# Attention scores of one head as one 32-row product on its own row group of TensorE, with the mask as a key row, in a fused cross-attention and expert kernel

## The reference, cut to what matters

```python
# x (64,128,128), ctx (64,120,128), mask (64,120); 16 heads of 8 dimensions, 8 experts of width 512
n = layernorm(x)
q, k, v = (n @ Wq + bq), (ctx @ Wk + bk), (ctx @ Wv + bv)         # split into 16 heads
score = einsum('bhqd,bhkd->bhqk', q, k) / sqrt(8)
score = where(mask, -1e30, score)
x = x + (softmax(score) @ v) @ Wo + bo
n = layernorm(x)
probs = softmax(n @ Wr.T); the two best of 8 experts, with their shares
x = x + sum over those two of share * (gelu(n @ W1[e] + b1[e]) @ W2[e] + b2[e])
```

## Time and profile before

| | us |
|---|---|
| median of 3 runs | 856.4 |
| lowest and highest run | 851.75, 870.18 |
| the profiled execution, its own time | 863.12 |
| its span, first to last instruction | 861.4 |

### The profile page before, as it was taken

How to read it: one execution, slowest core, us unless ns; L and a number is a source line. 1 busy time by engine, 2 the same in 40 slices (tenths; PEclk the granted TensorE clock), 3 DMA queues, 4 the chain that set the end, 5 groups by cost and what they waited for, 6 DMA issues and landing times.

```text
span 861.4 us, 18252 instructions
## 1 busy us (share of the span) xinstructions
PE 646.0 (75%) x4964; PEld 493.1 (57%) x4964; DVE 554.5 (64%) x1813; ACT 531.5 (62%) x1060; POOL 490.2 (57%) x892
## 2 busy tenths in 40 slices
PE   2677786876877888878978546999898979989400
PEld 1355565665655656655656435887686858767300
DVE  4466677776877778767866543766475656656436
ACT  4367676765866667767767435887576767866300
POOL 8233366655675757656677770675565646566610
PEclk9899999997999999999999758999899999999855
DMA  4666766667567776676665167877575756664068
GB/s 139 182 180 170 212 183 198 180 199 204 166 184 216 203 204 180 196 195 196 169 179 145 52 183 233 268 244 234 177 214 180 225 183 213 202 193 155 4 240 344
DMA packets 118905, 164.24 MB, mean 191 GB/s; under 512 B 22479, under 2 KB 77286, under 8 KB 118823
## 3 DMA queue, kind: packets, MB, share of 16 engines
q1 hardware_dynamic: 107143, 141.87, 56.4%
q0 software_dynamic: 9088, 17.07, 5.8%
q10 hardware_dynamic: 2592, 4.33, 1.3%
HBM read 73.07 MB, written 33.92 MB: 124 GB/s over the span
## 4 chain that ended last, share of the span: by engine, by line
PE 38%; SPq 17%; DMA 16%; issue 13%; POOL 6%; DVE 5%; ACT 2%; another core or an unknown queue 2%; POOLq 0%; DVEq 0%; ACTq 0%
DMA qb<-negm 4%; SPq L330 4%; DMA qb<-dense 4%; PE bank L1260 4%; SPq L312 4%; PE bank L1428 4%; PE bank L1426 3%; PE bank L1427 3%; PE bank L1411 3%; PE bank L1412 3%; PE bank L1414 3%; PE bank L1275 3%; DMA qb<-yd 3%; PE bank L1248 3%; SPq L338 2%
## 5 line engine op out<-in xcount | busy, mean ns | idle before, releaser
L650 POOL DMA_INDIRECT yd<-vs,idt x156 | 159.8, 1025 | 127.9 <-DVE vs L961 81.0
L1009 ACT ACTIVATE pt<-bank,mcol 120x512 f32<-120x512 f32 x256 | 167.9, 687 | 53.4 <-PE bank L1260 43.5
L707 DVE TENSOR_REDUCE mx<-bank 128x4 f32<-128x480 f32 x256 | 159.9, 649 | 46.0 <-PE bank L1248 39.3
L550 POOL DMA_INDIRECT xd<-rows,posi x128 | 128.7, 1005 | 98.2 <-DVE posi L812 68.4
L947 DVE TENSOR_TENSOR qb<-hid,qb 128x512 fp32r<-128x512 f32 x156 | 108.3, 694 | 101.4 <-ACT hid L1142 61.0
L1139 ACT ACTIVATE qb<-bank,btile 128x512 fp32r<-128x512 f32 x156 | 109.2, 700 | 72.4 <-PE bank L1428 42.1
L1260 PE MATMUL bank<-qb,dense 128*120 128x512 f32 x256 | 97.4, 460 | 61.2 <-DMA qb<-negm 50.7
L1248 PE MATMUL bank<-kb,dense 128*128 128x480 f32 x256 | 92.7, 445 | 22.7 <-issue 8.5
L1142 ACT ACTIVATE hid<-bank,btile 128x512 f32<-128x512 f32 x156 | 109.0, 699 | 0.0
L1041 ACT ACTIVATE ots<-bank 128x512 f32<-128x512 f32 x64 | 38.2, 597 | 79.0 <-PE bank L1275 71.0
L1260 PEld LDWEIGHTS bank<-qb,dense 128*120 128x120 f32 x256 | 39.7, 192 | 70.3 <-DMA qb<-negm 56.9
(11 more groups left out here) (169 smaller groups left out, 1559.0 us busy)
## 6 DMA issues: line engine op xcount, KB each, us to landing
kb<-wd SPq DMA_DIRECT2D x40, 512.0 KB
qb<-wd SPq DMA_DIRECT2D x38, 512.0 KB
qb<-dense SPq DMA_DIRECT2D x128, 128.0 KB
dense<-comp SPq DMA_DIRECT2D x64, 248.0 KB
kb<-dense SPq DMA_DIRECT2D x128, 120.0 KB
rows<-xd SPq DMA_DIRECT2D x39, 264.0 KB
wd<-wsp SPq DMA_DIRECT2D x16, 512.0 KB
qb<-yd SPq DMA_DIRECT2D x16, 512.0 KB, 6.2
```

The costliest lines, as they stand in the source:

```text
L550: g.indirect_dma_start(xd, bass.IndirectOffsetOnAxis(ap=posi[r % 4][:, bk:bk + 1], axis=0), rows[r % 4][:, bk // 2, bk % 2, :], None, boun ...
L650: g.indirect_dma_start(yd, bass.IndirectOffsetOnAxis(ap=idt[k][:, j:j + 1], axis=0), yrow[p.parity][:, j, :], None, bounds_check=2 * NTOK ...
L707: v.tensor_reduce(mx[c % 2][:, :, gg, b], wide[m % 2][:, 0:J * KL].rearrange("p (j k) -> p j k", j=J), op=ALU.max, axis=AX.X).then_inc(w_f ...
L1009: a.activation(pt[i % NP][:].rearrange("p j q -> p (j q)"), scores[t % 2][0:KL, :], ACT.Exp, bias=mcol[:, 2 * c + t // G:2 * c + t // G + ...
```

## The change

The block operands `kb` and `qb` are gone, with key_blocks, query_blocks and the zeroing. `dense` is split into `dq` and `dk`, four buffers of each. A head's product now contracts only its own 32 partitions, with `tile_position=(32j, 0)`, so on row group j of the array: 16 matmuls of 120 columns replace 4 by_query matmuls, 16 of 128 columns replace 4 by_key matmuls. A call makes 8 of them, alternating between two row groups, each of which writes its own bank; it waits until both banks have been read. The mask lies in row 11 of `dk` (one DMA, L320 before) and so enters both products, and the exponential has no bias. The maxima go to rows 31 and 15 of `dq`. As `dk` has ones in both rows at all times, row 15 (with 31, 47 and so on) of a reused `dq` is zeroed first by a small DMA (`cleared`). The parts of `comp` are spread by 6 DMAs where 4 did it. The expert stage gets buffers of its own, and its wait for the last by_key is gone. `best` and `exponential` see the same number of elements, with g and j exchanged.

```diff
-    NHI, NLO, MSK = 3, 7, 11
+    MSK, NLO, NHI = 11, 15, 31
-        dense = [sb(f"dense{k}", [P, G, NK], F32R) for k in range(ND)]
-        qb = [sb(f"qb{k}", [P, J, G, N2], F32R) for k in range(2)]
-        kb = [sb(f"kb{k}", [P, J, G, K2], F32R) for k in range(2)]
+        dq = [sb(f"dq{k}", [P, G, N2], F32R) for k in range(ND)]
+        dk = [sb(f"dk{k}", [P, G, K2], F32R) for k in range(ND)]
+        wt = sb("wt", [P, 4, 2, 2, HID], F32R)
+        xThl = sb("xThl", [P, 2, 2, TB], F32R)
+        hhl = sb("hhl", [P, 2, HC, TB], F32R)
...
-            def key_blocks(c):
...
-            def query_blocks(c):
...
+            def prepare(c):
                 if c < ND:
                     sp.wait_ge(dense_set, 2 * (c + 1))
                 else:
                     sp.wait_ge(b_full, 8 * (c - ND + 1))
+                    sp.dma_start(dq[c % ND][NLO::16]..., dq[c % ND][3::16]...).then_inc(cleared[c % ND], 16)
+                sp.dma_start(dk[c % ND][MSK::R]..., maskd...to_broadcast([J, G, K2])).then_inc(mask_row[c % ND], 16)
             def spread_high(c):
                 sp.wait_ge(hi_done, 2 * c + 1)
+                for term in (1, 2):
+                    sp.dma_start(rows_of(dq, c, term), comp[:, QHI]...).then_inc(dn_in[c % 2], 16)
                 sp.wait_ge(hi_done, 2 * c + 2)
+                for term in (0, 2):
+                    sp.dma_start(rows_of(dk, c, term), comp[:, KHI]...).then_inc(dn_in[c % 2], 16)
             def spread_low(c):
                 sp.wait_ge(lo_done, 2 * c + 1)
+                sp.dma_start(rows_of(dq, c, 0), comp[:, QLO]...)
                 sp.wait_ge(lo_done, 2 * c + 2)
+                sp.dma_start(rows_of(dk, c, 1), comp[:, KLO]...)
             def maxima(c):
                 sp.wait_ge(nm_split, 2 * c + 2)
-                sp.wait_ge(qblk[c % 2], 64 * (c // 2 + 1))
...
             def slot(n):                                  # SP
-                if chunk(n + 1):
-                    query_blocks(n + 1)
+                if chunk(n + 3):
+                    prepare(n + 3)
...
-                if chunk(n + 3):
-                    key_blocks(n + 3)
-                    mask_rows(n + 3)
...
-                    sp.wait_ge(b_full, 8 * NCH)           # before the third tile's weights
...
-            v.memset(flat(kb[0], "p j g n").bitcast(F32), 0.0).then_inc(kb_zero, 1)   # and kb[1]
-            clear(qb[0])                                  # ACT, and qb[1]
...
-                a.activation(pt..., scores[t % 2][0:KL, :], ACT.Exp, bias=mcol[:, ...], scale=SCALE)
+                a.activation(pt..., scores[t % 2][0:KL, :], ACT.Exp, scale=SCALE)
...
+            def by_query(c, p):
+                b, half = divmod(p, 2)
+                if p == 0:
+                    pe.wait_ge(dn_in[c % 2], 96 * (c // 2 + 1))
+                    pe.wait_ge(mask_row[c % ND], 16 * (c // ND + 1))
+                    if c >= ND:
+                        pe.wait_ge(cleared[c % ND], 16 * (c // ND))
+                m = 8 * c + 2 * p
+                if m:
+                    pe.wait_ge(w_free, m)
+                for g in range(G):
+                    for k in range(2):
+                        j = 2 * half + k
+                        last = t_.matmul(wide[k][:, g * KL:(g + 1) * KL], dq[c % ND][R * j:R * j + R, g, b * S:(b + 1) * S],
+                                         dk[c % ND][R * j:R * j + R, g, b * KL:(b + 1) * KL], start=True, stop=True, tile_position=(R * j, 0))
+                        if g == G - 1:
+                            last.then_inc(w_full, 1)
+            def by_key(c, p):                             # the same with dk as weights, dq moving,
...                                                       # scores[k], and a wait for exp_done 8c + 2p
             def slot(n):                                  # PE: one call where two matmuls stood
-                by_key(n, 0)
-                by_key(n, 1)
+                by_key(n, 0)
                 if chunk(n - 2):
                     project_out(2 * n - 3)
-                by_query(n + 1, 4)
-                by_query(n + 1, 5)
+                by_query(n + 1, 2)
```

More of the change, by code:

```diff
@@ L44, in turns, with moe_attention @@
         return self.quad * each + (each + more)
-def moe_attention(nc, x, ctx, mask, maskT, Wq, Wk, bqk, Wv, bv, Wo, bo, Wr, W1, b12, W2, out):
+def moe_attention(nc, x, ctx, mask, Wq, Wk, bqk, Wv, bv, Wo, bo, Wr, W1, b12, W2, out):
     S, B, D = x.shape
@@ L104, in moe_attention @@
         bias_qk = sb("bias_qk", [P, 2])
-        ones_k = sb("ones_k", [P, 1])
+        pad_q = sb("pad_q", [P, 1])
+        pad_k = [sb(f"pad_k{i}", [P, 1]) for i in range(3)]
         masku = sb("masku", [B, KL], mask.dtype)
@@ L176, in moe_attention @@
         flat = lambda t, spec: t[:].rearrange(f"{spec} -> p ({spec[2:]})")
[L177 to L182, removed]
+        wtile = [wt[:, k] for k in range(4)]
+        xTh, xTl = ([xThl[:, k, i, :] for k in range(2)] for i in range(2))
         xrow = [rows[k][:].rearrange("p a b w -> p (a b) w") for k in range(4)]
@@ L211, in moe_attention @@
         w_full, w_free = sem("w_full"), sem("w_free")
-        dn_in, qblk, kblk, kfirst, mrow = two("dn_in"), two("qblk"), two("kblk"), two("kfirst"), two("mrow")
+        dn_in, cleared, mrow = two("dn_in"), four("cleared"), two("mrow")
         v_full, v_taken = sem("v_full"), sem("v_taken")
@@ L290, in spread_high @@
                     sp.wait_ge(b_full, 8 * (c - ND + 1))
[L291 to L302, removed]
@@ L304, in key_blocks @@
-            def key_blocks(c):
[L306 to L315, removed]
+                    sp.dma_start(dq[c % ND][NLO::16].rearrange("x g n -> x (g n)").bitcast(F32),
+                                 dq[c % ND][3::16].rearrange("x g n -> x (g n)").bitcast(F32)).then_inc(cleared[c % ND], 16)
@@ L1252, in by_key @@
+            def by_key(c, p):
                 if not chunk(c):
                     return
-                b, g = divmod(t, G)
-                i = 8 * c + t
-                if t == 0:
+                b, half = divmod(p, 2)
+                if p == 0:
                     pe.wait_ge(mrow[c % 2], 32 * (c // 2 + 1))
-                if i >= 2:
-                    pe.wait_ge(exp_done, i - 1)
-                t_.matmul(scores[t % 2][0:KL, :].rearrange("p (j q) -> p j q", j=J), dense[c % ND][:, g, N2 + b * KL:N2 + (b + 1) * KL],
-                          qb[c % 2][:, :, g, b * S:(b + 1) * S], start=True, stop=True).then_inc(b_full, 1)
+                i = 8 * c + 2 * p
+                if i:
+                    pe.wait_ge(exp_done, i)
+                for g in range(G):
+                    for k in range(2):
+                        j = 2 * half + k
+                        last = t_.matmul(scores[k][0:KL, g * S:(g + 1) * S], dk[c % ND][R * j:R * j + R, g, b * KL:(b + 1) * KL],
+                                         dq[c % ND][R * j:R * j + R, g, b * S:(b + 1) * S], start=True, stop=True, tile_position=(R * j, 0))
+                        if g == G - 1:
+                            last.then_inc(b_full, 1)
@@ L1341, in slot @@
                     earlier(n - 4)
-                by_key(n, 2)
-                by_key(n, 3)
-                by_query(n + 1, 6)
-                by_query(n + 1, 7)
+                by_key(n, 1)
+                by_query(n + 1, 3)
                 if chunk(n - 1):
@@ L1352, in slot @@
                     turn_heads(2 * n - 1)
-                by_key(n, 4)
-                by_key(n, 5)
+                by_key(n, 2)
                 if chunk(n + 1):
@@ L1358, in slot @@
                 by_query(n + 2, 0)
-                by_query(n + 2, 1)
                 if chunk(n):
@@ L1365, in slot @@
                     values(n + 1)
-                by_key(n, 6)
-                by_key(n, 7)
-                by_query(n + 2, 2)
-                by_query(n + 2, 3)
+                by_key(n, 3)
+                by_query(n + 2, 1)
                 if chunk(n - 1):
```

102 lines of the change are left out of this document (42 added, 60 removed).

## The result

| | before, us | after, us |
|---|---|---|
| median of 5 runs each, same chip | 857.45 | 943.57 |
| lowest and highest | 851.75, 870.18 | 934.02, 969.00 |
| the profiled execution | 863.12 | 969.00 |

The ratio is 1.095 (95% interval 1.084 to 1.106): the change makes the kernel slower.

What follows compares the result with a forecast made beforehand. SP's queue was taken as the bound, with PE behind it. 32 slots x (13.7 - 12.7) = 32 us and 6 for filling gave -38: 825 us profiled, 818 for the median; range 795 to 880.

Steps and rivals of the forecast that it cites:

- The clock falls: Rival: tiled calls get half clock for a third of each slot, PE needs +3.5 us, about 930 us; chance 0.04.
- the forecast's 12.7: Attention slot length in us: the dense slot's 11.4 plus 1.3 for PE, against a mean of 13.7 before.
- SP, 12.5 to 7.3 us: SP's queue per slot: 5 fewer issues (3.2 us) and 2 us less waiting, so SP stops being the bound.
- Maxima a wait of 0.2 us, put at nothing: Before by_key: maxima land 5.3 us after q high, PE needs them after 5.1; the wait counted as nothing.
- "5.1": Time in us from `high` writing q to the next by_key: 4.45 plus what PE gains in calls.
- Row groups load side by side, 0.45 us a call: PE: weight loads of two row groups overlap, so a call's 8 products take 4 x 0.112 = 0.45 us.
- PE +1.3 us a slot: PE's by_key and by_query calls, with drains and bare loads at mode switches, cost 1.3 us more a slot.
- Filling -6 us: Before the first by_key: by_query starts about 3.7 us sooner and maxima are issued sooner, 6 us gained in all.
- Waits in SP's place: Rival: waits for both banks or late maxima cost 1.0 us a slot, only filling is gained, 850 us; chance 0.17.
- PE busy without a gap in slots above 14: One of the trace signs named in advance as showing the forecast wrong, in the attention slots.
- loads going one by one: Rival: the two row groups' weight loads don't overlap, +3.6 us, slots of 16.3 us, 933 us; chance 0.10.

Runs made afterwards that it cites:

- g5: The changed kernel (after), unedited, run again on the second chip as a control: 862.2 us, ratio 1.047 to before.
- E2: After with each call making two all-row products in place of eight row-group products, scores not the reference's: 760.1 us, ratio 0.930 to before.
- e1: Separate kernel, PE alone running patterns of row-group and all-row products: two groups with 128 columns took 64.8 us at clock 0.53.
- g6: After with each row-group product streaming 240 or 256 columns in place of 120 or 128, half the scores wrong: 811.6 us, ratio 0.987 to before.
- h9: e4 with the keys' spreads issued after the maxima and `earlier` moved behind the second call, third chip: 866.6 us.
- h11: g6 with the same two order edits as h9, third chip: 870.2 us, ratio 1.016 to before.
- h10: e4 unedited, run again on the third chip as a control: 889.4 us, ratio 1.043 to before.
- e4: After with each by_key call and the by_query call behind it merged into 16 products over four row groups, first chip: 780.9 us, ratio 0.954 to before.
- e3: After with one useless all-row product added to each of its 8 calls a slot: 952.8 us, ratio 1.163 to before.
- g7: After with by_query in two all-row products a call and by_key left on row groups: 779.5 us, ratio 0.951 to before.

## Why the prediction was wrong, point by point

The step that failed is the rival "The clock falls", to which I gave 0.04. Its price came out near, by luck: half clock for a third of each slot, +3.5 us, about 930 us. Measured: half clock for 64% of the stage, slots of 16.9 against the forecast's 12.7, so +4.2 us, and 943.6 us. In the prediction's own sum 3.5 us of work take 7.0 of 16.2 us, so half clock would have been 43% of the time. Two errors met: there was more half clock, and less beside it, for with the clock at 1.00 a slot of 16.9 us would come to 16.9 x (1 - 0.64 / 2) = 11.5 us, not 12.7 (an estimate, as if PE bounded all of it). Its chance was wrong, and so were "nothing but the risk" for it, where two of the three stretches of the earlier trace rows already stand at 0.93 and 0.90, and the one piece of evidence against it, "in the dense slot with its tiled `weigh` the clock stays at 1.00". `Weigh` feeds 120 rows into four column groups. It was no neighbour of products that use 32 rows of each of two groups. The rows before held no such product, so what the clock would do was an unknown cost like the others and should have been bounded from both sides. The earlier trace rows had the dear end, a `weigh` of 1.94 us against 1.08; with PE as the bound behind SP, it applies to all of a slot, and such slots took 20.16 us.

The other steps, against the rows of after and g5:

- **SP, 12.5 to 7.3 us: right.** The slot's issues in after, timeline of SP's queue:

```profile
269.38 1.22 SPq L302 DMA_DIRECT2D dq<-comp  x2
270.64 1.50 SPq L305 DMA_DIRECT2D dk<-comp  x2
272.20 1.19 SPq L318 DMA_DIRECT2D dq<-negm  x2
...
276.02 0.83 SPq L292 DMA_DIRECT2D dk<-maskd  x1
```

  From 269.38 to 276.85 are 7.5 us; then SP waits.
- **Maxima a wait of 0.2 us, put at nothing: small, as forecast.** Counted as in the earlier trace rows, they are waited for 7.3 us in all of after and 14.1 in g5, where 14.1 / 32 = 0.4 a slot. The 0.2 itself holds a slip: between 414.04 and 418.49 PE's calls get longer by 0.10 + 0.28, not by the 0.65 behind "5.1", so the sum should have given 4.8 and a wait of 0.5.
- **Row groups load side by side, 0.45 us a call: right** (0.47 for by_key, 0.53 for by_query).
- **PE +1.3 us a slot: too much, if anything.** In g5's slot of 13.05 us the clock of 0.87 means 3.4 us at half, which at full clock would be 1.7: PE is busy 12.69 - 1.7 = 11.0 us, against 10.58 in before's slot at 1.00. That is +0.4 of busy time; drains between matmuls that overlap a modelled end aren't in it. The 13.05 us are near the forecast's 12.7 even with that half clock in them. If all slots were like this one, 31 x 0.8 = 25 us would be gained on the 13.8 of before.
- **Filling -6 us: -2.8.** By_query starts at 20.49 us, 3.4 sooner than in the earlier trace rows, but each call now waits for two reductions, and the maxima are ready only 0.4 us sooner:

```profile
20.49 1.11 PE L1219 MATMUL bank<-dk,dq 32*128 32x120 f32 x8 [1.08 <-DMA dk<-comp]
23.43 1.11 PE L1219 MATMUL bank<-dk,dq 32*128 32x120 f32 x8 [1.83 <-DVE mx L682]
```

- **Waits in SP's place: small.** For exponentials PE waits 1.5 us in all of after and 5.8 in g5, for reductions 4.9 in either. The waits for `taken` are 21.3 us, but they aren't new: in before they are 17.3. E2 has the same waits for two banks and slots of 11.8 us.
- **"PE busy without a gap in slots above 14"** was named as the sign of a wrong forecast, and it is what the trace shows. I had tied it to loads going one by one; the half clock gives the same picture, and only the clock column and the durations of untouched matmuls tell the two apart.

**Shown:** the two-group, 128-column pattern alone takes the clock to half with PE never idle (e1); in the kernel longer streams of the same products bring it from 0.75 to 0.95 and gain 51 us net (g6), without a stall in either run; all-row products, which can't keep the heads apart, keep it at 0.99, and the time is then 7% under before (e2). **Argued only:** what the chip measures when it lowers the clock. **Open:** what stalls the engines in after and in h9 to h11; how much of after's loss (1.095 against g5's 1.047) and of h10's lower clock (0.77 against e4's 0.89) comes from those stalls and how much from the chip otherwise; and why e3's filler brought the clock back so little where g6's columns did.

## What to carry to other kernels

Before splitting an all-row matmul into products on row groups, ask what the new pattern does to the granted clock, and measure the pattern by itself between stretches of all-row work: a busy PE isn't a PE at 2.4 GHz, and half clock slows the untouched work as well. If you use row groups, stream long (g6) or keep the other products at all rows (g7). Four groups at once kept the full clock by themselves (e1), but in the kernel that version was faster on one chip and slower on another. Where a gain hangs on the clock, run it on more than one chip, and look for stalls that come from outside the kernel before you compare two traces.

## What the runs showed of the hardware

- Granted clock of 0.53 and 0.55 in stretches where PE was busy for 64.8 and 47.8 us without a gap (e1), after 25.6 and 74.3 us at full clock.
- Four row groups take 640 products in 18.09 us, 0.028 each, so 4 x 0.028 = 0.113 us for a group: 32-row loads of four groups overlap as well as those of two.
- Identical programs differ by chip more than by most edits: before 817, 820 and 852 us, at the same clock; after's ratio 1.095 and 1.047; e4's kernel 0.954 and 1.043.
- On the chips where before takes 852 us and more, the traces show stalls of ScalarE or VectorE of some 2 to 3 us that are ended from outside the profile: 14 of VectorE in after, 24 and 23 of the two in h10. The traces of the other two chips show none.
